# Sixteen attention cores on one NeuronCore: another order of the first steps, and four shifts inside head groups

## The reference, cut to what matters

```python
x = x + _layernorm(_L0_attn_ref(_layernorm(x), w_qkv, w_o))
x = x + _layernorm(_L0_ffn_ref(_layernorm(x), ...))

# _L0_attn_ref
qkv = (x @ w_qkv).reshape(B, T, 3, NH, HD)
q = rotary_apply(q, cos, sin); k = rotary_apply(k, cos, sin)
scores = einsum('bhqd,bhkd->bhqk', q, k) / sqrt(HD)
attn = softmax(where(causal, scores, -inf))
out = einsum('bhqk,bhkd->bqhd', attn, v) @ w_o

# _L0_ffn_ref
h = x + attention(rmsnorm(x, ln1_w), ...)   # q from x @ q_d_w, k and v from x @ kv_d_w, rotated half of k from x @ rope_k_w
out = h + moe(rmsnorm(h, ln2_w), ...)       # a shared expert and the top 2 of 7
```

## Time and profile before

| what | value |
|---|---|
| median of 3 runs | 2364.48 us (2362.02 to 2365.16) |
| profiled execution, its own time | 2375.47 us |
| its span | 2373.6 us |
| PE busy in it | 2125.7 us (90%) |
| VectorE, ScalarE, GpSimd busy | 1549.9, 1068.3, 1066.9 us |
| mean granted TensorE clock | 0.953 |

### The profile page before, as it was taken

How to read it: one execution, slowest core, us unless ns; L and a number is a source line. 1 busy time by engine, 2 the same in 40 slices (tenths; PEclk the granted TensorE clock), 3 DMA queues, 4 the chain that set the end, 5 groups by cost and what they waited for, 6 DMA issues and landing times. The chain is left out here.

```text
span 2373.6 us, 38332 instructions
## 1 busy us (share of the span) xinstructions
PE 2125.7 (90%) x12880; PEld 1516.8 (64%) x12880; DVE 1549.9 (65%) x4272; ACT 1068.3 (45%) x2166; POOL 1066.9 (45%) x1092
## 2 busy tenths in 40 slices
PE   5799989999989999998999999898597999999993
PEld 4576565766756667665666766553365788888872
DVE  5676767677666776666777676774475555665557
ACT  2345454434554433445443355542332455555543
POOL 1445654455564444645545455543255133333322
PEclk9999999999999999998999999997799999999997
DMA  5554456544555645554656455342566788877896
GB/s 165 161 135 143 143 160 206 152 143 116 167 155 172 177 135 153 152 150 126 179 164 183 126 154 141 108 124 56 204 223 236 228 209 211 195 194 188 216 270 222
DMA packets 226527, 400.00 MB, mean 169 GB/s; under 512 B 25118, under 2 KB 95646, under 8 KB 222238
## 3 DMA queue, kind: packets, MB, share of 16 engines
q1 hardware_dynamic: 162590, 297.86, 42.6%
q0 software_dynamic: 17792, 39.99, 8.7%
q10 hardware_dynamic: 45952, 59.71, 7.0%
HBM read 147.85 MB, written 148.44 MB: 125 GB/s over the span
## 5 line engine op out<-in xcount | busy, mean ns | idle before, releaser
L939 DVE CUSTOM_DVE_ANT_0 unused<-score,mask 128x128 bf16<-128x128 f32 (+3 forms) x1024 | 467.8, 486 | 275.4 <-PE score L1171 255.3
L725 ACT ACTIVATE probs<-scoresT 128x512 f32<-128x512 f32 (+3 forms) x1024 | 426.8, 437 | 463.5 <-PE scoresT L1194 449.0
L1194 PE MATMUL scoresT<-stacks 97*128 97x256 f32 (+2 forms) x1024 | 402.1, 408 | 35.4 <-ACT probs L725 26.8
L639 POOL TENSOR_TENSOR probs<-probs 128x1536 f32<-128x1536 f32 (+1 forms) x128 | 374.9, 2929 | 38.4 <-PE out_ps L1208 29.3
L1171 PE MATMUL score<-stacks 96*128 96x256 f32 (+2 forms) x1024 | 350.6, 387 | 29.8 <-DVE rowmax L939 28.1
L628 POOL TENSOR_SCALAR_AFFINE_SELECT probs<-probs 128x512 f32<-128x512 f32 x256 | 163.8, 640 | 368.0 <-ACT probs L725 367.8
L1194 PEld LDWEIGHTS scoresT<-stacks 97*128 97x128 f32 x1024 | 196.6, 195 | 163.3 <-ACT probs L725 96.4
L1171 PEld LDWEIGHTS score<-stacks 96*128 96x128 f32 x1024 | 185.1, 197 | 166.0 <-issue 125.1
L1836 POOL DMA_INDIRECT h_summed<-y,goal x88 | 141.4, 1607 | 294.2 <-ACT y L1932 274.1
L1233 PE MATMUL middle<-wo,outT 128*128 128x512 f32 x512 | 259.5, 597 | 0.0
L956 DVE RECIPROCAL total<-sum_ps 128x128 f32<-128x128 f32 x256 | 235.1, 938 | 36.3 <-PE sum_ps L1219 31.8
(11 more groups left out here) (196 smaller groups left out, 4046.7 us busy)
## 6 DMA issues: line engine op xcount, KB each, us to landing
stacks<-parts SPq DMA_DIRECT2D x768, 128.0 KB, 2.4
x_slots<-mask ACTq DMA_DIRECT2D x56, 1032.0 KB, 5.2
xr<-x_slots SPq DMA_DIRECT2D x22, 1032.0 KB
wturn<-parts_kept SPq DMA_DIRECT2D x7, 2048.0 KB, 8.6
raw<-in_gates SPq DMA_DIRECT2D x24, 512.0 KB
raw<-in_ups SPq DMA_DIRECT2D x24, 512.0 KB
raw<-in_downs SPq DMA_DIRECT2D x24, 512.0 KB
normed<-in_L_attn_x SPq DMA_DIRECT2D x8, 1024.0 KB, 6.2
```

The costliest lines, as they stand in the source:

```text
L639: pool.tensor_tensor(probs[0][:, :, P * j:T], probs[0][:, :, P * j:T], probs[j][:, :, :], ALU.add)\
L725: act.activation(probs[j][:, h, 0:width], scoresT[:, u % ST_BANKS, first:first + width], ACT.Exp, scale=SCALE).then_inc(exp_done, 1)
L939: ins = dve.tensor_tensor_reduce(unused[t][:, :], score.bank(name)[:, first:first + width], mask[:, T - width:T], 1.0, MASKED, ALU.add, AL ...
L1194: pe.matmul(scoresT[:, u % ST_BANKS, 0:T - first], heads[0:ROWMAX + 1, 1, h, j * P:(j + 1) * P], heads[0:ROWMAX + 1, 0, h, first:T], start ...
```

## The change

The tables and lists that make the step order are edited; the set of steps and the arithmetic are the same.

- First steps: XT of the first rows stands ahead of the weight splits WQ, where it stood behind them. PE's first projection waits for the first four low parts, and its second quarter for all eight. WV stands behind T(0,1), where it stood ahead of P(1,0). The eight quarters of the first values stand singly between parts of S(0), where they stood in two blocks of four. The load of the value weights counts on `turn_in`, and ACT waits for it at WV alone.
- Kinds 0 and 3, g = 1: the third part of the values (V, c, 3) stands behind Y and behind `own`, the projections of group 4c + 3, which T at this group's end transposes; it stood ahead of both.
- Kind 1, g = 1: `own` stands ahead of the values, where it stood behind them and WT; WT is last.
- Kind 2, g = 1: the first norm steps stand behind six fillers (were four), the next behind ten (were eight).
- Kind 1, g = 2: LAT, LAT, q projection, first rotated keys KR, norms XI, plain keys KU, second KR; before it was LAT, KR, XI, KR, q projection, LAT, KU.

```diff
-G1_AT = {1: (6, 12), 2: (4, 8)}
+G1_AT = {1: (6, 12), 2: (6, 10)}
...
-            steps = turned + quarters("V", c, 3) + y[3] + own + ([("HS", f)] if ends else [])
+            steps = turned + y[3] + own + quarters("V", c, 3) + ([("HS", f)] if ends else [])
...
-        ahead = values + turned + own
+        ahead = own + values + turned if kind == 1 else values + turned + own
...
-                return (quarters("LAT", p, 1) + keys[:4] + written + keys[4:] + q + quarters("LAT", p, 0) + k)
+                return (quarters("LAT", p, 1) + quarters("LAT", p, 0) + q + keys[:4] + written + k + keys[4:])
...
-                *(("WQ", k) for k in range(2 * CT)), *(("XT", 0, k) for k in range(CT)), *quarters("P", 0, 0),
-                *quarters("P", 0, 1), ("NL", 1), *(("WV", k) for k in range(CT)),
-                *quarters("P", 1, 0), ("T", 0, 0), ("T", 0, 1), *quarters("P", 1, 1)]
+                *(("XT", 0, k) for k in range(CT)), *(("WQ", k) for k in range(2 * CT)), *quarters("P", 0, 0),
+                *quarters("P", 0, 1), ("NL", 1), *quarters("P", 1, 0), ("T", 0, 0), ("T", 0, 1),
+                *(("WV", k) for k in range(CT)), *quarters("P", 1, 1)]
+    values = quarters("V", 0, 0) + quarters("V", 0, 1)
     for h in range(GH):
-        yield from [("S", 0, h, part) for part in range(3)]
-        if h < 2:
-            yield from quarters("V", 0, h)
+        for part in range(3):
+            yield "S", 0, h, part
+            if part < 2:
+                yield values.pop(0)
...
-                    sp.dma_start(probs[0][:, :, :], columns[:, :, 2 * D:3 * D]).then_inc(qkv_in, 16)
+                    sp.dma_start(probs[0][:, :, :], columns[:, :, 2 * D:3 * D]).then_inc(turn_in, 16)
...
-                            act.wait_ge(qkv_in, 16 * 2)
+                            act.wait_ge(qkv_in, 16)
...
+                        if k == 0:
+                            act.wait_ge(turn_in, 16)
...
-                        pe.wait_ge(turn_in, 16 * (p // 2))
+                        pe.wait_ge(turn_in, 16 * (p // 2 + 1))
...
-                    if step == "P" and which == [0, 0, 0]:
-                        pe.wait_ge(weights_low, 2 * CT)
+                    if step == "P" and which in ([0, 0, 0], [0, 0, 1]):
+                        pe.wait_ge(weights_low, CT * (which[2] + 1))
```

## The result

| kernel | median of its runs, us | lowest to highest | ratio to before [95% interval] |
|---|---|---|---|
| before, beside it | 2364.51 (6 runs) | 2359.55 to 2368.32 | |
| changed | 2345.57 (6 runs) | 2334.59 to 2351.93 | 0.9917 [0.9895, 0.9939] |
| before, on a second chip | 2374.41 (29 runs) | 2368.25 to 2384.45 | |
| changed, on the second chip | 2349.76 (6 runs) | 2343.06 to 2360.53 | 0.9877 [0.9853, 0.9902] |

The change gives 19 us by the first pair of medians, 25 by the second; the forecast was 30. The two profiles therefore show 40.9 us, twice what the first medians show, and have to be read with that in mind.

A forecast was written before the change was run, and what follows sets the result against it. PE, busy 90% of the span, bounds the kernel by work, waits and low clock. Waits 24.1 plus clock 6.3 make 30.4 us, taken from the median of 2364.48: 2334 us, range 2320 to 2350.

The forecast's parts named there:

- Start, 5.8: First steps up to T(1): first score 3.2 us earlier, 2.6 us of waits between scores filled by single value quarters; 5.8 us.
- T in kind 0, 10.2: End of g = 1 in kind 0: PE's wait at T for POOL's rotated keys nearly goes; 2.4 + 3 x 2.6 us.
- Kind 1, g = 1, 4.0: Four groups: the score's 1.01 us wait for DVE's maxima goes, as the rotation moves to the group's start; 4 x 1.0 us.
- Kind 1, g = 2, -2.4: Four groups: waits of 0.51 + 0.36 go, a new 1.6 us wait comes at T(8,1); 4 x 0.6 us lost.
- The first rival: Clock doesn't come back: waits alone, less four new low stretches behind T(8) at half of 1.9 us; 2344 us, chance 0.18.
- Kind 2, 1.8: Four groups: one exponential now ahead of ACT's norm shortens PE's 3.45 us wait at ST by 0.45 each; 1.8 us.
- Kind 3, 3.3, and core 15, 1.4: Score's 1.48 us wait for maxima behind DVE's rotation and column: 3 x 1.1 us won in kind 3, 1.4 in core 15.
- that rotation comes about 2 us sooner: Kind 3, DVE: with Y and the projection ahead of the values, the rotation delaying the maxima starts about 2 us earlier.
- The waits, 24.1: All PE waits won at the places touched, 26.5 us, less 2.4 lost in kind 1's g = 2: 24.1 us.
- The clock, 6.3: Low-clock stretches returning to full clock where waits go: 12.6 us if all return, half taken, 6.3 us.
- The theory: Attention part: a PE wait costs its own length and sometimes a stretch at 1.2 GHz behind it; 24.1 + 6.3 us gain.
- The rival, that the low stretches only move and the sum is the waits alone: Clock doesn't come back: low stretches return in other places, leaving the waits' 24.1 us; put at 2344 us, chance 0.18.

## Why the prediction was right, and where it was not

The time lies in the range and on the forecast side, 12 us above the number: the waits that went came to less than forecast, and the clock's share, a guess between nothing and 12.6, was near by luck. By its steps:

- **Start, 5.8.** Right: 5.4 in the idle time, 5.9 [2.4, 9.5] by the ratio of the start alone. The 3.2 before the first score came as 3.45 (46.90 to 43.45), the 2.6 between the scores as 2.64. The largest wait of this group, 5.75 us for DVE at a score of group 1, was not touched and stands at 5.78.
- **T in kind 0, 10.2.** Nearly right: 7.0 of 7.8 in groups 17, 33 and 49. Group 1 gave 1.6, not 2.4: its wait at T is gone, but a score now waits 0.51 and a PV 0.25. In the kind 0 groups PV waited for POOL's masks 0.25 at most.
- **Kind 1, g = 1, 4.0.** The wait of 1.01 went in all four groups, but 0.49 for ACT at the last scoresT of the group took part of its place: 2.7. The late reload of `wturn` cost nothing; the latents of kind 1's g = 2 waited for nothing in any profile.
- **Kind 1, g = 2, -2.4.** Mis-sized, and with the clock behind it the term that failed most. In the idle time it is -4.2, as above: the chain was right at 2.42 but the work that PE has to cover it with was counted as 0.8 and is 0.6, its start behind POOL took 0.26 more, and the 0.6 I took for the net was below my own 0.7. Behind it comes the clock, which the sum had at nothing: groups 6, 7 and their like took 10.3 us more, where the idle time makes 3.7. Alone this part measured 8.0 us [4.5, 11.4]. The first rival had this mechanism, at 4 us for four stretches.
- **Kind 2, 1.8.** Right: 1.9. In group 9 the 3.45 of the earlier trace rows became three waits, together 3.08 where the forecast was 3.0. PE's timeline there in the changed kernel:

```profile
293.81 0.70 PE L1198 MATMUL scoresT<-stacks 97*128 97x512 f32 x1 [1.62 <-ACT probs L727]
...
295.67 1.17 PE L1198 MATMUL scoresT<-stacks 97*128 97x512 f32 x2 [1.15 <-ACT probs L727]
...
297.14 0.69 PE L1198 MATMUL scoresT<-stacks 97*128 97x384 f32 x1 [0.31 <-ACT probs L727]
```

- **Kind 3, 3.3, and core 15, 1.4.** Wrong: 0.1 and 0.1. The step that failed is "that rotation comes about 2 us sooner": it came 1.2 us sooner (7.2 us into group 29 instead of 8.4), and in its new place it stands behind other work that I had not counted. Timelines of group 29 in the changed kernel, DVE, then PE:

```profile
782.07 1.31 DVE L851 TENSOR_SCALAR normed<-normed,meanvar,rstd 128x512 f32<-128x512 f32 x2
783.30 0.94 DVE L960 RECIPROCAL total<-sum_ps 128x128 f32<-128x128 f32 x1
784.16 0.35 DVE L889 COPY qk<-middle 128x256 f32<-128x256 f32 x1
```

```profile
785.35 0.66 PE L1050 MATMUL middle<-ident,normed 128*128 128x128 f32 x4 [1.19 <-DVEq L894]
...
788.46 0.47 PE L1175 MATMUL score<-stacks 96*128 96x256 f32 x2 [0.55 <-DVE rowmax L943]
```

  The rotation starts with the copy at 784.16, behind two norms and a reciprocal, and PE's next transposes need the bank that it frees: 1.19 + 0.55 instead of 1.48. In groups 13 and 45 it was 1.21 + 0.29, and a PV there waited 0.39 for POOL. With the norms ahead the 1.19 is gone in all three groups (62.7 us for the three instead of 66.1), so they, and not ACT's copy or the reciprocal, which still stands there, held that bank; 0.55 at the score stays. For core 15 the wait went from 1.48 to 1.24 only; its cause was not tried.
- **The waits, 24.1.** 15.6 in the profile: 1.6 too much in kind 0, 1.3 in kind 1's g = 1, 1.8 in its g = 2, 4.5 in kind 3 and core 15.
- **The clock, 6.3.** The attention part alone became 24.0 us shorter, so 24.0 - 15.6 = 8.4 is the clock, or 3 by the first pair of medians and 9 by the second. The 15.6 is of one pair of profiles; the pair without the expert part has 13.1, which would leave 10.9. Half of 12.6 was about right, but not for the reason given. In the g = 1 groups of kinds 0, 1 and 3 the clock came back in full: with the waits that is 9.8 us in kind 1 and 13.2 in kind 0. In the pair of profiles of the whole kernels the clock gave 20.5 us in the groups where waits went and took 8.6 in the others, most of it in and behind kind 1's g = 2.

**The theory**, that PE's waits cost their own length and part of a low stretch, holds. The rival, that the low stretches only move and the sum is the waits alone, fits kind 1's g = 1: 2.6 us [-0.9, 6.4] with 3.4 less idle time in all, though the interval leaves room for 3 us of clock. It does not hold for the new wait in kind 1's g = 2, with 8.0 [4.5, 11.4] against 3.9 of idle time, nor for kind 2, with 6.6 [3.3, 9.9] against 1.6. For kinds 0 and 3, with 12.3 [8.3, 16.3] against 8.8, the measurement does not decide. The Trainium skill, "TensorE: Matmul & The Clock Gate", "What's actually happening", says that the monitor behind the clock runs freely, so that its changes fall differently from run to run; the two profiles of the changed kernel agree, with nearly one idle time (124.9 and 123.7) and 11.1 us between their attention parts.

The five parts alone make -5.9 + 8.0 - 6.6 - 12.3 - 2.6 = -19.4 us; the whole gave -19.6 by the first ratio and -29 by the second. So they add up within what the measurement can tell, the second only just: the intervals are 3 to 4 us to either side for each part and 5 to 6 for the whole.

**Open.** Why group 25 and its like ran at 0.78 in some executions and 0.88 in others, why groups 7, 23, 39 and 55 had a low clock in 13 of 40 cases without the long wait, and why the expert part took between 710.9 and 730.4 us in the profiles of the whole kernels. That the waits ahead of a fall cause it was not tried apart from the order of the steps.

## What to carry to other kernels

Before a step is moved, list what its result needs on every other engine and put a filler behind the step that starts the longest such chain: a rotation of 2.4 us over two engines needs 2.4 us of PE's own work between it and its reader, and the four quarters of plain keys, which stood there before, brought the wait from 2.04 down to 0.78. Count also what already stands in the queue at the new place; in kind 3 two norms there took back nearly all of the gain. Book the waits in full, and the granted clock of single groups at well under what they show: a group whose clock comes back may hand the low stretch to another, and only the whole kernel's time, over many runs, tells how much is left.

## What the runs showed of the hardware

- Most waits repeat and the clock does not. The wait of 2.04 us at T was the same in sixteen groups of four profiles; group 7 had 17.5 to 20.0 us and a granted clock of 0.84 to 1.00 with the same order in it. Waits for a small DMA do vary: a scoresT of group 33 waited 0.44 us for one in the changed kernel and 0.60 in the same attention part without the experts.
- With the wait of 2.04 us the clock fell more often, from its own group into the next, and the two groups lost more than the wait: 10.3 us over four pairs of groups between the two profiles, 3.7 of them idle time, and 10.4 against 3.9 in the means of 4 and 10 profiles.
- In unchanged code that follows the attention part, profiles differ by up to 19.5 us (710.9 and 730.4). A profile of one execution may so lie 11 us to either side of its kernel's median, and two of them can show twice the difference of the medians.
